# The gates of two graphs as one 2x2 block product with seven block products

## The reference

```
for each graph:
  weight[d] = (adj == d) / (count of d in the row + EPS)      d = 1..4
  agg  = concat over d of weight[d] @ hid                     [128, 4*256]
  out  = relu(agg @ Wd.T + bd)
  r = sigmoid(out @ Wri.T + bri + hid @ Wrh.T + brh)
  z = sigmoid(out @ Wzi.T + bzi + hid @ Wzh.T + bzh)
  n = tanh(out @ Wni.T + bni + r * (hid @ Wnh.T + bnh))
  res = (1 - z) * n + z * hid
  result = layernorm(res) * gamma + beta
```

## Time and profile before

| | |
|---|---|
| median of 3 runs | 555.54 us (554.86 to 555.58) |
| the profiled execution | 554.72 us, its span in the profile 552.9 us |
| TensorE matmul | busy 97% of the span, 3202 matmuls |
| VectorE | 77%, 1018 instructions |
| ScalarE | 49%, 588 |
| GpSimd | 46%, 394 |
| granted clock of TensorE, mean | 0.997 |
| moved by DMA | 33.41 MB, 60 GB/s in the mean |

### The profile page before, as it was taken

How to read it: one execution, slowest core, us unless ns; L and a number is a source line. 1 busy time by engine, 2 the same in 40 slices (tenths; PEclk the granted TensorE clock), 3 DMA queues, 4 the chain that set the end, 5 groups by cost and what they waited for, 6 DMA issues and landing times.

```text
span 552.9 us, 10278 instructions
## 1 busy us (share of the span) xinstructions
PE 536.0 (97%) x3202; PEld 458.4 (83%) x3203; DVE 425.8 (77%) x1018; ACT 268.7 (49%) x588; POOL 252.1 (46%) x394
## 2 busy tenths in 40 slices
PE   5899999999999999999999999999999999999994
PEld 3688888888888888888888888888888888888883
DVE  4878877877877877877877877877877877876776
ACT  4644454454454454454454454454454454454442
POOL 2624445444444444444444444444444444444433
PEclk9999999999999999999999999999999999999998
DMA  7502030111203012030111103012030111102001
GB/s 260 223 2 78 21 104 20 58 68 58 67 19 114 15 51 76 18 105 19 57 66 57 67 18 101 25 53 76 16 107 19 57 67 57 51 17 59 20 10 39
DMA packets 23812, 33.41 MB, mean 60 GB/s; under 512 B 1952, under 2 KB 19104, under 8 KB 23664
## 3 DMA queue, kind: packets, MB, share of 16 engines
q1 hardware_dynamic: 23680, 32.84, 18.1%
q0 software_dynamic: 112, 0.33, 0.2%
HBM read 24.77 MB, written 8.39 MB: 60 GB/s over the span
## 4 chain that ended last, share of the span: by engine, by line
PE 93%; DMA 2%; issue 1%; SPq 1%; ACT 1%; DVE 1%; POOL 0%; POOLq 0%; another core or an unknown queue 0%; DVEq 0%; ACTq 0%
PE y_bank L284 31%; PE rz_bank L284 31%; PE n_bank L284 16%; PE p_bank L379 11%; PE out_bank L363 2%; DMA vec_rows<-in_vectors 2%; PE count_bank L328 1%; SPq L185 0%; PE p_bank L284 0%; POOL wg_lo L657 0%; SPq L245 0%; ACT n_bank L408 0%; DVE pre_n L532 0%; DVE rn_sb L524 0%; ACT n_sb L432 0%
## 5 line engine op out<-in xcount | busy, mean ns | idle before, releaser
L284 PE MATMUL y_bank<-wd_hi,xT_hi 128*128 128x512 f32 x256 | 102.1, 399 | 4.8 <-ACT wd_hi L416 4.8
L284 PE MATMUL y_bank<-wd_lo,xT_hi 128*128 128x512 f32 x256 | 102.0, 398 | 0.0
L284 PE MATMUL y_bank<-wd_hi,xT_lo 128*128 128x512 f32 x256 | 101.3, 396 | 0.0
L452 ACT ACTIVATE oT_hi<-out_bank 128x256 fp32r<-128x256 f32 x64 | 24.6, 385 | 156.0 <-PE out_bank L363 156.0
L514 DVE SCALAR_TENSOR_TENSOR out_rows<-p_bank,rcount,out_rows 128x256 f32<-128x256 f32 x192 | 91.7, 478 | 2.4
L677 POOL TENSOR_TENSOR var_eps<-mean_var,ln_eps 128x1 f32<-128x1 f32 x64 | 12.3, 193 | 175.6 <-DVE mean_var L621 175.6
L563 DVE TENSOR_TENSOR y_lo<-y_bank,y_hi 128x512 fp32r<-128x512 f32 x128 | 87.2, 681 | 2.0 <-ACT y_hi L440 0.9
L425 ACT ACTIVATE y_hi<-y_bank 128x512 fp32r<-128x512 f32 x64 | 38.2, 597 | 98.3 <-PE y_bank L284 98.3
L665 POOL TENSOR_TENSOR by_gamma<-scaled,vec_rows 128x256 f32<-128x256 f32 x61 | 45.2, 741 | 86.8 <-DVE scaled L549 86.8
L514 DVE SCALAR_TENSOR_TENSOR out_rows<-p_bank,rcount,bd_rows 128x256 f32<-128x256 f32 x64 | 31.0, 484 | 57.9 <-PE p_bank L379 57.8
L379 PE MATMUL p_bank<-y_hi,masks 128*128 128x256 f32 x256 | 63.8, 282 | 1.0 <-DVE y_lo L563 1.0
(11 more groups left out here) (105 smaller groups left out, 1340.3 us busy)
## 6 DMA issues: line engine op xcount, KB each, us to landing
x_in<-in_x SPq DMA_DIRECT2D x16, 512.0 KB, 3.8
out<-normed SPq DMA_DIRECT2D x64, 128.0 KB, 1.7
xT_f<-in_xT SPq DMA_DIRECT2D x15, 512.0 KB, 3.3
adjT_in<-in_adjT SPq DMA_DIRECT2D x15, 256.0 KB, 3.3
wg_f<-in_wgT SPq DMA_DIRECT2D x2, 768.0 KB, 8.7
vec_rows<-in_vectors SPq DMA_DIRECT2D x1, 1024.0 KB, 12.0
wd_f<-in_wdT SPq DMA_DIRECT2D x3, 256.0 KB, 5.6
xT_f<-in_xT SPq DMA_DIRECT2D x1, 384.0 KB, 6.4
```

The lines of the kernel that those rows point to most:

```text
L284: last = nc.tensor.matmul(dst, m[:, c, :], w[:, c, w_at], start=(first and c == 0 and t == 0), stop=(final and c == HC - 1 and t == 2), sk ...
L452: nc.scalar.activation(oT_hi[:, (i - 1) % OT_RING, :, :], src, ACT.Relu).then_inc(ohi_ready, 1)
```

## The change

The program works on pairs of graphs. `step(i)` is played for i = 0 to 34, with six steps unrolled, a loop of six rounds of four, and the rest unrolled; the gates lag by two steps, the mix by three, the normalisation by four.

The gates of a pair are seen as one matrix product of 2x2 blocks. The rows of blocks are the two graphs; the inner index is the half of the features; the columns of blocks are two sets of 384 weight columns, one with a half of n and r, the other with the other half of n and z. Seven block products (the Winograd form of Strassen's scheme) stand for eight. It needs sums of the blocks of x and of `out` (S1 to S4) and of the weights (T1 to T4), three passes for each product, and sums of the products (U2, U3 and the four C blocks). The part of a product on x fills columns 0 to 383 of a bank, the part on `out` adds to columns 128 to 511, so that both n parts stay apart while r or z is summed.

What each engine has new, beside the work on 512 instead of 256 columns:

- TensorE: 42 matmuls of 384 columns a pair for 24 of 512 and 24 of 256. The label sums come in two steps: labels 1 and 3 first, then, after ScalarE has scaled the banks' content by the ratio of counts, labels 2 and 4 on top. The counts are made for each pair.
- ScalarE: that scaling (four instructions), the split of the x sums and o sums, relu of `out` for the o sums (back into the bank), the filling of `alpha` and `gamma` with biases, the seed of `beta` as a copy of `alpha`, and the copies U2, U3, C11, C21. One sigmoid over r and z of both graphs from SBUF.
- VectorE: two label scalings a graph for four; the sums of the o blocks; C12 and C22; masks by four scalar comparisons a pair, each on 256 columns; the whole normalisation, from a `mix` that stands in PSUM.
- GpSimd: the sums of the x blocks and their lo part, the lo part of the o sums, and x - n and z times it.
- Before the first gates: T1 to T4 of both weight sets (VectorE and GpSimd), and hi and lo of 14 blocks of 384 columns (12 chunks of 256 columns, in six pieces of 512, before).
- The loads of x, adj and rows and the stores go by pairs. The special ways of the last three graphs are gone.

```diff
-                    passes(rz[:, :], x_hi, x_lo, slice(2 * H, 4 * H), wg_hi, wg_lo, False, False, seeded=True)
-                    passes(rz[:, :], o_hi, o_lo, slice(0, 2 * H), wg_hi, wg_lo, False, True, seeded=True)\
-                    passes(n_part[:, 0:H], x_hi, x_lo, slice(5 * H, 6 * H), wg_hi, wg_lo, False, False, seeded=True)
-                    passes(n_part[:, H:2 * H], o_hi, o_lo, slice(4 * H, 5 * H), wg_hi, wg_lo, False, True, seeded=True)\
...
+                def p_part(k, g, second):
+                    at = 2 * k + g
+                    if second:
+                        pe.wait_ge(p_scaled, up(2 * at + 2, 4))
+                    else:
+                        pe.wait_ge(ylo_ready[0], up(at + 1, 2))
+                        pe.wait_ge(ylo_ready[1], up(at + 1, 2))
+                        if at >= 1:
+                            pe.wait_ge(out_ready, up(at, 2))
...
+                def product(dst, left, w):
+                    slot = q % XRING
+                    three_passes(dst[:, 0:GATE], x_hi[:, slot, left, :], x_lo[:, slot, left, :],
+                                 wx_hi[:, w, :], wx_lo[:, w, :])
+                    if q == 0 and w <= B22:
+                        pe.wait_ge(wo_plain_ready, 1)
+                    elif q == 0:
+                        pe.wait_ge(wo_sums_ready, w - B22)
+                    if w <= B22 and left != S4:
+                        pe.wait_ge(olo_ready, up(q + 1))
+                    else:
+                        pe.wait_ge(oslo_ready, up(q + 1))
+                    return three_passes(dst[:, 128:512], o_hi[:, q % 2, left - 1, :], o_lo[:, q % 2, left - 1, :],
+                                        wo_hi[:, w, :], wo_lo[:, w, :])
...
+                y(0, 0)
+                if has_pair(q):
+                    if q == 0:
+                        pe.wait_ge(wx_ready, 2)
+                    pe.wait_ge(alpha_loaded, up(q + 1))
+                    product(alpha, A11, B11).then_inc(p1_done, 1)
+                if has_pair(i - 1):
+                    p_part(i - 1, 1, True)
+                if has_pair(q):
+                    pe.wait_ge(xslo_ready, up(q + 1))
+                    pe.wait_ge(gamma_loaded, up(q + 1))
+                    product(gamma, S1, T1).then_inc(p5_done, 1)
+                y(0, 1)
+                if has_pair(i - 1):
+                    pe.wait_ge(out_ready, up(2 * i, 2))
+                    if i < PAIRS:
+                        pe.wait_ge(counts_ready, up(i + 1))
+                    for g in range(2):
+                        for c in range(HC):
+                            last = nc.tensor.transpose(t_bank[:, (2 * g + c) * N:(2 * g + c + 1) * N],
+                                                       out_rows[:, g, c * N:(c + 1) * N], ident[:, :])
+                    last.then_inc(t_done, 1)
+                if has_pair(q):
+                    pe.wait_ge(beta_seeded, up(q + 1))
+                    product(alpha, S2, T2).then_inc(p6_done, 1)
+                    product(beta, A12, B21).then_inc(p2_done, 1)
+                if i == 0:
+                    count(0)
+                if has_pair(i):
+                    p_part(i, 0, False)
+                y(1, 0)
+                if has_pair(q):
+                    pe.wait_ge(u2_ready, up(q + 1))
+                    product(alpha, S3, T3).then_inc(p7_done, 1)
+                if has_pair(i):
+                    p_part(i, 0, True)
+                y(1, 1)
+                if has_pair(q):
+                    pe.wait_ge(u3_ready, up(q + 1))
+                    product(alpha, A22, T4).then_inc(p4_done, 1)
+                    pe.wait_ge(c22_ready, up(q + 1))
+                    product(gamma, S4, B22).then_inc(p3_done, 1)
+                if has_pair(i):
+                    p_part(i, 1, False)
+                if has_pair(i + 1):
+                    count(i + 1)
```

VectorE's masks and SyncE's waits:

```diff
+        def label_masks(k, d):
+
+            src = adj_in[:, k % 2, :].rearrange("p (g m) -> p g m", g=2)
+            return masks[:, k % 2, :, d, :], src, float(d + 1), None, ALU.is_equal
...
+                if has_pair(i + 2):
+
+                    sp.wait_ge(xsum_ready, up(3 * i + 3, 3))
+                    load_x(i, up(i + 2))
+                    sp.wait_ge(masks_ready, up(D * (i + 1), D))
+                    load_adj(i, up(i + 2))
...
+                    if k >= 2:
+                        sp.wait_ge(from_ready, up(k - 1))
...
+                    sp.wait_ge(result_ready, up(2 * j + 2, 2))
```

More of the change, by code:

```diff
@@ L46, in gnn_kernel @@
+        wo_lo = sb("wo_lo", [128, WBLOCKS, GATE], f32r)
         ident = sb("ident", [128, 128])
         ones_bf = sb("ones_bf", [128, 1], bf16)
-        labels = sb("labels", [128, D, N])
+        zeros_bf = sb("zeros_bf", [128, 512], bf16)
         bd_rows = sb("bd_rows", [128, H])
[L50 to L53, removed]
@@ L66, in gnn_kernel @@
[L66 to L77, removed]
@@ new lines, in gnn_kernel @@
+        x_lo = sb("x_lo", [128, XRING, 8, N], f32r)
+        adj_in = sb("adj_in", [128, 2, 2 * N], i32)
+        x_rows = sb("x_rows", [128, 2, 2, H])
+        masks = sb("masks", [128, 2, 2, D, N], f32r)
+        y_hi = sb("y_hi", [128, 2, D * H], f32r)
+        y_lo = sb("y_lo", [128, 2, D * H], f32r)
+        counts = sb("counts", [128, 2, 2, D])
+        rcount = sb("rcount", [128, 2, 2, D])
+        ratio = sb("ratio", [128, 2, 2, 2])
+        out_rows = sb("out_rows", [128, 2, H])
+        o_sums = sb("o_sums", [128, 5, N])
@@ new lines, in gnn_kernel @@
+        more_vec = x_rows[:, :, :, :].rearrange("p k g f -> p (k g f)")
+        y_bank = [bank("y_bank0"), bank("y_bank1")]
+        p_bank = bank("p_bank")
+        alpha = bank("alpha")
+        beta = bank("beta")
+        gamma = bank("gamma")
+        t_bank = bank("t_bank")
+        mix = bank("mix")
+        x_loaded = [sem("x_loaded0"), sem("x_loaded1")]
+        adj0_loaded = sem("adj0_loaded")
+        adj_loaded = [sem("adj_loaded0"), sem("adj_loaded1")]
+        rows_loaded = [sem("rows_loaded0"), sem("rows_loaded1")]
@@ L290, in _ @@
             pe.wait_ge(zeros_ready, 1)
-            nc.tensor.matmul(rz_bank[:, :], zeros_bf[:, 0:128], zeros_bf[:, :], start=True, stop=True)
-            nc.tensor.matmul(n_bank[:, :], zeros_bf[:, 0:128], zeros_bf[:, :], start=True, stop=True)\
-                .then_inc(banks_marked, 1)
+            for dst in (alpha, beta, gamma):
+                marked = nc.tensor.matmul(dst[:, :], zeros_bf[:, 0:128], zeros_bf[:, :], start=True, stop=True)
+            marked.then_inc(banks_marked, 1)
             pe.wait_ge(const_ready, 1)
@@ new lines, in step @@
+                if has_pair(q):
+                    act.wait_ge(p6_done, up(q + 1))
+                    if q >= 1:
+                        act.wait_ge(c12_ready, up(q))
+                    nc.scalar.activation(u2_sb[:, :], alpha[:, :], ACT.Copy).then_inc(u2_ready, 1)
+                    act.wait_ge(p2_done, up(q + 1))
+                    if q >= 1:
+                        act.wait_ge(pre_ready, up(q))
+                        act.wait_ge(rz_ready, up(q))
+                    nc.scalar.activation(c_sb[:, 1, 0, :], beta[:, :], ACT.Copy).then_inc(c11_ready, 1)
@@ L537, in step @@
+                y_low(0, 0)
                 if i == 1:
                     dve.wait_ge(bd_loaded, 16)
[L539 to L551 removed]
@@ new lines, in gate_blocks @@
+    def gate_blocks(gates, n, gate_first):
+        blocks = []
+        for c, side in ((0, 0), (1, 0), (1, 1), (0, 1)):
+            parts = [chunk(n, c)[:, side * 128:(side + 1) * 128], chunk(gates[side], c)]
+            blocks.append(np.concatenate(parts[::-1] if gate_first else parts, axis=1))
+        return np.concatenate(blocks, axis=1)
+    xT = np.asarray(x).reshape(PAIRS, 2, N, HC, 128).transpose(0, 4, 1, 3, 2).reshape(PAIRS, 128, 2 * HC * N)
+    adjT = np.asarray(adj).reshape(PAIRS, 2, N, N).transpose(0, 3, 1, 2).reshape(PAIRS, N, 2 * N)
```

946 lines of the change are left out of this document (517 added, 429 removed).

## The result

| | before | after |
|---|---|---|
| median | 555.56 us (554.86 to 555.78) | 564.88 us (563.84 to 565.31, 4 runs) |
| span of the profiled execution | 552.9 us | 563.0 us |
| matmuls | 3202 | 3011 |
| granted clock, mean | 0.997 | 0.984 |

The ratio of after to before is 1.0169, interval [1.0156, 1.0181]. The forecast of 539.6 us, faster, was wrong, and its range ended at 558.

A forecast was written before the change was run, and what follows sets the result against it. TensorE, busy 97% of the span, was taken to bound the kernel. 32 x 1.0 = 32 us gained, 16 given back at both ends, gave 539.6 us; own range 533 to 548, outer ends 530 and 558.

The forecast's parts named there:

- TensorE's gain: Gates of two graphs on TensorE: 42 matmuls of 384 columns at 0.176 take 7.39 us instead of 8.44, gaining 1.05.
- VectorE's sum: VectorE's work for a pair: 15.0 us of durations, 13.0 after overlaps, 2.6 us to spare within 15.6.
- the walk: Engine-by-engine schedule of one steady pair: 15.6 us without a stall, thinnest margin 0.6 us at the last y_lo.
- r times n and its addition 1.4: On VectorE, the product of r with n and the following addition were put at 1.4 us a pair together.
- only mix and the product with r read two SBUF tensors: Argument against GpSimd delaying VectorE: just these two VectorE operations have two SBUF inputs.
- The row above shows no such rate: VectorE's masks: 0.404 each from the nearest profiled form, 1.6 a pair, instead of the skill's doubled-rate 0.28.
- the first sign of being wrong: On TensorE, label sums waiting for y_lo in every pair would show the forecast wrong.
- GpSimd holds VectorE up: Masks and mix wait for GpSimd's block sums and z product: slip 2.0, 580 us; decisive from 1.15; chance 0.19.
- The start: Before steady pairs: first product at 8.2 us, waits for weight preparation, a clock loss of 1.4; step 3 begins at 52.1.
- The drain: After TensorE's last matmul, nothing hides the last pair's work: 13.6 us to the span's end, against 7.3 before.
- The preparation hides better: At the start, weight pieces overlap between VectorE and ScalarE, without the waits of step 1: 533 us; chance 0.13.
- The narrower matmuls gain nothing: On TensorE, 384 columns cost as much as 512, 9.77 us a pair: 616 us; chance 0.01.

The follow-up runs named there:

- e6: On the kernel with early masks (e1), the product A12 B21 was computed and added twice, eight products a pair: 576.31 us.
- e7: On e1, GpSimd takes the first three `wo_lo` blocks at the start, and its lo part of pair 2's x sums goes behind `o_lo`: 545.14 us.
- e12: On e1 with the last pair's x - n and z product on VectorE, GpSimd's T sums of wo moved from step 0 to step 1: 543.33 us.
- e1: On the changed kernel, VectorE's four masks of the next pair moved ahead of the sums of the o blocks: 544.56 us.
- e9: On the changed kernel, the masks put behind the second label sum of the pair before, ahead of r times n: 554.68 us.

## Why the prediction was wrong

**TensorE's gain was right.** The matmul of 384 columns is 0.175 (forecast 0.176), the pair without a stall 15.56 (forecast 15.6), and an eighth product costs 1.05 in a steady pair, the gain that I had on the gates.

**The step that failed** is VectorE's sum and the walk built on it. The walk had one margin, 0.6 us at the last `y_lo`, and named it as the thinnest. The wait came at just that place. Two terms were mis-sized.
- "r times n and its addition 1.4" measured 0.69 + 1.55. I wrote that "only mix and the product with r read two SBUF tensors". The addition does too: its `c_sb` is a copy in SBUF, where the addition of before read a PSUM bank. And it, not the product, meets `x_lo`.
- The masks, 0.404 each by the nearest row, measured 0.551. The block took 2.12; my walk had 1.3. The row L549 is a form with two pointer operands (scalars taken from a column) and two operations. With no pointer a mask alone takes 0.285, with one 0.348, so a pointer costs 0.06, and 0.404 fits two of them. That the second operation costs nothing is not shown. "The row above shows no such rate" was read from a form that is not the masks'. The masks were cheaper than I thought when alone, and dearer beside GpSimd.

Some 0.85 and 0.8 us, less the margin of 0.6, make a stall of 1.05 a pair; the profile shows 0.86 in the pair at 300 us (16.42 less 15.56) and 0.74 in the mean (16.30 less 15.56). It was the first sign of being wrong that the prediction named, label sums that wait for `y_lo` in every pair. The price of the wait for the relu, 0.75 in my walk and 1.02 in the trace, was in the forecast; that it could be filled was not seen.

**The rival "GpSimd holds VectorE up" was right**, with a chance of 0.19. It had the mechanism and the point from which it decides, a slip of 1.15. The slip was the margin of 0.6 and the stall of 0.74, 1.3, just past it: steps 3 to 31 alone, with 19.2 us more than forecast, take back the 15.9 us of gain and 3.3 more, and the other 6.8 of the 26.0 lie at the two ends. Against it I had held that "only mix" and the product read two SBUF tensors and that the earlier trace rows show a part of a delay only. Those rows were a warning: the masks of before took 0.85 beside GpSimd and 0.68 the first time, and I scaled neither to the new forms. It named the wrong pair of operations (masks and mix with the block sums) for half of the loss. The mix takes 0.689 and is not touched in the changed kernel.
By the Trainium skill (SBUF — State Buffer, Who interferes with whom) a VectorE operation with two SBUF inputs and a GpSimd operation that reads SBUF exclude each other for the whole instruction. The trace agrees: L643 begins 0.19 behind `x_lo`, and ends 0.55 behind `x_lo`'s end, where an addition alone takes 0.69. By the Trainium skill (VectorE: DVE Perf Modes, The perf-mode tier table) a mask alone would be 0.28, an estimate from the doubled rate of fp32 in SBUF. The trace agrees, with int32 in: L564 shows 0.285.

**The ends.** The start cost 4.4 more than walked: VectorE's and GpSimd's sums of weights beside each other, `wo_lo` 5.8 for 4.4, and waits of TensorE that took the clock down for a part of 20 to 40 us, 1.2 us on one y group (forecast 1.4 for the clock). The first gates began at 40.7, where I had 34. Steps 32 and 33 cost 2.4 more, in waits, most of them for U2 and U3. The drain was right, 13.5 for 13.6. e6 shows the price of both ends together: 21 us, of which I had 16.

**"The preparation hides better"** did not happen, and e7 and e12 did not bring it about. "The narrower matmuls gain nothing" is refuted by 0.175.

**Still open.** Which order is best I only found by trial: early masks, a late `x_lo` and both gave -20, -1 and +7 us against after. That e1's gain is the filled wait is read from the idle column; no run took the wait away in another way. Why step 3 begins later in e9 is not followed, and for e12 the wait of ScalarE is read from the trace alone. A mask that reads PSUM, which should meet nothing, was not tried.

## What to carry to other kernels

A scheme that trades matrix work for sums moves work to engines that may exclude each other: count the elementwise operations with no PSUM operand, take their duration from rows beside a running GpSimd operation, and compare with the slack at the last hand-over to TensorE, not with the engine's busy share. When one engine is late by a microsecond, look first for an idle stretch in its own order that an independent operation can fill; that gained 20 us here, while taking single meetings away moved the time by -1, +7 and -10. Count a coarser step's two ends for themselves: here they ate two thirds of the saving.

## What the runs showed of the hardware

- VectorE operations whose tensors all lie in SBUF and GpSimd's tensor operations hold each other up. VectorE: 512-column additions 0.69 alone, 1.55 met; masks 0.285 alone, 0.54 to 0.89 in the mean when met. GpSimd's sum of 128 columns (L767) takes 0.46 alone and 0.928 in the mean.
- Operations on the same engine that read PSUM are not held up: `y_lo` is 0.678 in the mean over 128, with GpSimd busy beside it or not.
- A scalar taken from a column costs about 0.06 us on VectorE's 256 columns (a mask alone 0.285 without, 0.348 with one; L549 with two, and a second operation, 0.404). On ScalarE the scaling of 256 columns takes 0.457 where the earlier trace rows has 0.385 without one; the scaling also writes to PSUM, which no run separates.
